# State 11 of a sixteen-state scan is summed in place on VectorE instead of being transposed on TensorE, with all instruction orders laid anew

## The reference

```python
proj = einsum('blh,he->bel', xn, W_in);  hidden, gate = split(proj, 2, axis=1)
hidden = silu(conv(hidden, conv_kernel) + conv_bias)          # 4 taps along the tokens
dt, Bm, Cm = split(einsum('ble,ed->bld', hs_ble, W_x), [128, 144], axis=-1)
dts = softplus(einsum('blr,re->ble', dt, W_dt) + b_dt)
dA  = exp(dts[..., None] * A);   dBu = dts[..., None] * Bm[:, :, None, :] * hs_ble[..., None]
def step(state, inp):                                         # along the 256 tokens
    a, bu, c = inp
    state = a * state + bu
    return state, einsum('ben,bn->be', state, c)              # sum over the 16 states
y = (scan_out + hidden * D) * silu(gate);   ssm = einsum('bel,eh->blh', y, W_out)
# moe: softmax router, top 8 of 32 renormalised; per expert (silu(x @ wg) * (x @ wu)) @ wd * weight
```

## Time and profile before

| | |
|---|---|
| median of three runs | 1346.49 us |
| the profiled execution | 1342.44 us |
| its span, first to last instruction | 1340.6 us |
| PE / PEld busy | 1301.6 / 1219.6 us (97% / 91%) |
| DVE / ACT / POOL busy | 1239.6 / 1213.2 / 1233.9 us (92% / 90% / 92%) |
| mean granted TensorE clock | 0.999 of 2.4 GHz |
| DMA | 130 GB/s mean |

### The profile page before, as it was taken

The page is one execution under the profiler, slowest core; times in us unless marked ns, Lnnn a source line. Parts: engine busy times, 40 slices in busy tenths (PEclk is TensorE's granted clock), DMA queues, the critical chain, the costliest instruction groups (busy, mean ns, idle before and its releaser), DMA issues.

```text
span 1340.6 us, 26644 instructions
## 1 busy us (share of the span) xinstructions
PE 1301.6 (97%) x9222; PEld 1219.6 (91%) x9222; DVE 1239.6 (92%) x1644; ACT 1213.2 (90%) x2111; POOL 1233.9 (92%) x674
## 2 busy tenths in 40 slices
PE   6899999999999999999999999999999999999998
PEld 5889999999999999999999999999999899999987
DVE  3799999999999999999999999999999999999997
ACT  5879999999999999999999999999999899999984
POOL 2999999999999989999999999989999999999996
PEclk9999999999999999999999999999999999999999
DMA  7543443544444344443544444344443534434342
GB/s 193 160 144 118 143 120 115 152 115 132 139 127 135 112 136 127 139 120 118 149 120 126 136 128 138 114 132 131 139 122 116 148 114 134 139 113 142 109 146 80
DMA packets 189399, 174.95 MB, mean 130 GB/s; under 512 B 43185, under 2 KB 172241, under 8 KB 189265
## 3 DMA queue, kind: packets, MB, share of 16 engines
q1 hardware_dynamic: 150864, 121.86, 30.5%
q10 hardware_dynamic: 38400, 51.40, 13.6%
HBM read 167.92 MB, written 5.24 MB: 129 GB/s over the span
## 4 chain that ended last, share of the span: by engine, by line
POOL 27%; issue 21%; ACT 19%; DVE 18%; PE 12%; DMA 2%; ACTq 1%; SPq 0%; DVEq 0%; POOLq 0%
POOL state L571 14%; POOL moe L586 6%; ACT decay L657 5%; PE pair_ps L1003 5%; ACT L657 5%; ACT L665 4%; DVE state L878 4%; PE out_ps L1138 3%; POOL state L580 3%; DVE dt L865 3%; DVE u L891 2%; DVE decay L878 2%; DVE u L919 2%; ACT moe L665 2%; DVE moe L898 2%
## 5 line engine op out<-in xcount | busy, mean ns | idle before, releaser
L571 POOL TENSOR_TENSOR state<-du,b_rep 128x1024 f32<-128x1024 f32 x256 | 611.7, 2395 | 61.1 <-DVE u L891 59.3
L878 DVE TENSOR_TENSOR_SCAN state<-decay,state 128x512 f32<-128x512 f32 x448 | 534.2, 1212 | 21.1 <-ACT decay L657 16.4
L657 ACT ACTIVATE decay<-dt,neg_a 128x255 f32<-128x255 f32 x1024 | 436.7, 465 | 37.7 <-DVE state L878 19.0
L1138 PE MATMUL out_ps<-w_down,moe 128*128 128x256 f32 x1536 | 355.9, 381 | 3.1 <-POOL moe L586 1.9
L1138 PEld LDWEIGHTS out_ps<-w_down,moe 128*128 128x128 f32 x1536 | 282.5, 190 | 38.6 <-issue 4.1
L586 POOL TENSOR_TENSOR moe<-moe,rw_rep 128x512 f32<-128x512 f32 x192 | 249.3, 1309 | 8.7 <-DVE moe L898 7.3
L580 POOL TENSOR_TENSOR state<-state,c_rep 128x1024 f32<-128x1024 f32 x96 | 244.1, 2543 | 1.6 <-DVE state L878 1.6
L1003 PE MATMUL pair_ps<-xnT_hi,w_gate_hi 128*128 128x256 f32 x768 | 228.9, 298 | 3.2 <-DVE moe L898 3.2
L1003 PE MATMUL pair_ps<-xnT_hi,w_up_hi 128*128 128x256 f32 x768 | 225.7, 294 | 2.8 <-ACT moe L665 1.9
L657 ACT ACT_TABLE_LOAD x171 | 219.4, 1283 | 2.5
L1003 PE MATMUL pair_ps<-xnT_lo,w_gate_hi 128*128 128x256 f32 x768 | 216.4, 282 | 0.0
(11 more groups left out here) (149 smaller groups left out, 2252.5 us busy)
## 6 DMA issues: line engine op xcount, KB each, us to landing
w_down<-in_L_ffn_w_down_dram SPq DMA_DIRECT2D x384, 128.0 KB, 2.9
b_rep<-b_dram ACTq DMA_DIRECT2D x128, 256.0 KB, 3.3
rw_rep<-rw_dram SPq DMA_DIRECT2D x256, 96.0 KB, 2.7
c_rep<-b_dram ACTq DMA_DIRECT2D x128, 128.0 KB, 3.3
rw_rep<-rw_dram SPq DMA_DIRECT2D x256, 64.0 KB, 2.6
rw_rep<-rw_dram SPq DMA_DIRECT2D x256, 32.0 KB, 2.6
x_in<-L_attn_input_states_dram SPq DMA_DIRECT2D x16, 256.0 KB, 3.8
res<-L_attn_input_states_dram SPq DMA_DIRECT2D x16, 256.0 KB, 3.1
```

The lines of the kernel that those rows point to most:

```text
L571: pool.tensor_tensor(state[:, n % STATES, :, :], du2[:, q, :, :], b_rep[:, n // BCH % 2, n % BCH, :][:, None, :].broadcast_to([P, ET, T]), ...
L657: last = act.activation(decay[:, h, j, 1:T], dt[:, q, e, 1:T], ACT.Exp, scale=neg_a[:, e, n:n + 1])
L878: dve.tensor_tensor_scan(a if n in ROWS_BY_VECTOR else x, a, x, 0.0, ALU.mult, ALU.add).then_inc(scanned, 1)
L1138: last = pe.matmul(out_ps[:, c, :], moe[:, p % RING, j, c * P:(c + 1) * P], w_down[:, p % RING, j, :], start=(p == 0 and j == 0 and c == 0 ...
```

## The change

State 11 is no longer turned: it joins states 5 and 9 as a row summed by VectorE in the decays' banks. Nine states are then not turned. The code is the same except for the lists; every order table has new numbers. The middle rows (blocks 1 to 14) and the parts for block 0 that are spoken of below:

```diff
-    BY_ROW = [n for n in range(NS) if n in ((2, 4, 5, 6, 8, 9, 10, 12))]
+    BY_ROW = [n for n in range(NS) if n in ((2, 4, 5, 6, 8, 9, 10, 11, 12))]
...
-    UNIT_AT = [[-48, -22, -8, 3, 22, 27, 27, 36, 37, 47, 51, 63, 63, 66, 72, 81, 81, 87, 96, 102, 108, 113, 113, 115],
-               [-3, -2, 4, 23, 26, 30, 30, 35, 36, 42, 45, 49, 49, 52, 55, 81, 85, 95, 101, 104, 108, 108, 114, 115],
...
-    OUT_AT = [[32, 34, 38, 53, 71, 85, 92, 108, 110, 115, 137, 140],
-              [32, 32, 41, 42, 69, 72, 89, 106, 110, 112, 137, 140],
...
-    TURN_AT = [[[1, 8], [23, 27], [28, 31], [68, 68], [95, 104], [105, 111], [114, 114], [117, 119]],
-               [[6, 6], [17, 19], [34, 34], [60, 69], [93, 94], [107, 108], [109, 109], [116, 116]],
...
-    TURN_Y_AT, PROJECT_AT = [[128, 131], [130, 132], [227, 242]], [156, 153, 255]
...
-    SILU_AT = [[-42, -26, 23, 39, 52, 55, 64, 74, 96, 99, 111, 115],
-               [-1, 12, 28, 39, 43, 55, 62, 71, 96, 97, 117, 120],
...
-    SCALAR_FRONT = [{'xnT': -105, 'hid0': -104, 'hid1': -95, 'weightsT': -1, 'low': -65, 'lowT': -49, 'dt0': -41, 'dt1': -35},
-                    {'xnT': -116, 'hid0': -108, 'hid1': -91, 'weightsT': -57, 'low': -50, 'lowT': -41, 'dt0': -40, 'dt1': -23},
...
-    SCALAR_ALONE = [{'conv_silu': -74, 'router_exp': -94, 'softplus': -29, 'first_state': 4, 'skip': -9, 'normed': -123, 'share': -45},
-                    {'conv_silu': -73, 'router_exp': -84, 'softplus': -20, 'first_state': 7, 'skip': 23, 'normed': -122, 'share': -62},
...
-    MUL_AT = [[-10, 13, 41, 55, 60, 67, 79, 85, 108, 112, 118, 124],
-              [14, 23, 41, 46, 59, 63, 79, 92, 107, 108, 127, 129],
...
-    ADD_AT = [[[23, 26], [58, 71], [81, 97], [104, 113], [113, 117], [121, 124], [126, 129]],
-              [[20, 22], [64, 65], [84, 98], [104, 105], [114, 116], [120, 126], [130, 131]],
...
-    ROW_ADD_AT = [[42, 54, [45, 47], 70, 80, [76, 79], 106, 116], [37, 49, [44, 47], 61, 78, [76, 76], 102, 119], [30, 51, [43, 44], 64, 78, [75, 76], 102, 153]]
-    VECTOR_ALONE = [{'stats': -127, 'lo': -99, 'logits': -57, 'route': -37, 'taps0': -80, 'taps1': -53, 'total': 162},
-                    {'stats': -125, 'lo': -107, 'logits': -79, 'route': -71, 'taps0': -98, 'taps1': -83, 'total': 165},
...
-    SUM_AT = [[136, 136], [135, 136], [201, 214]]
...
-    WEIGH_AT = [[25, 26, 36, 43, 56, 65, 73, 94, 102, 110, 135, 136],
-                [17, 29, 37, 44, 65, 66, 80, 91, 99, 103, 131, 133],
...
-    ROW_MUL_AT = [[17, 30, [44, 44], 42, 63, [75, 78], 86, 91], [21, 32, [43, 45], 55, 67, [72, 76], 90, 92], [12, 30, [42, 44], 49, 67, [73, 76], 89, 116]]
-    POOL_ALONE = [{'rstd': -120, 'step_input': -35, 'gated': 142, 'select': -95},
-                  {'rstd': -127, 'step_input': -17, 'gated': 140, 'select': -66},
...
-    C_LOAD_AT = [[-11, 7, 26, 43, 44, 62, 69, 86], [-10, -10, 26, 40, 41, 61, 70, 80], [-22, -22, 31, 43, 57, 63, 82, 92]]
-    ROWS_BY_VECTOR = [n for n in BY_ROW if n in ((5, 9))]
+    UNIT_AT = [[-63, -27, -15, -7, 8, 18, 27, 42, 42, 44, 51, 51, 57, 57, 65, 74, 76, 76, 89, 90, 92, 99, 110, 114],
+               [-5, -4, -2, 16, 21, 24, 37, 37, 39, 51, 51, 52, 58, 61, 74, 75, 93, 94, 101, 102, 102, 111, 114, 122],
...
+    OUT_AT = [[29, 32, 49, 56, 61, 67, 85, 97, 99, 112, 139, 140],
+              [32, 40, 41, 65, 67, 77, 83, 97, 109, 112, 141, 142],
...
+    TURN_AT = [[[6, 10], [14, 15], [17, 31], [63, 74], [104, 107], [111, 112], [120, 123]],
+               [[5, 6], [15, 16], [30, 32], [73, 74], [104, 108], [111, 112], [118, 122]],
...
+    TURN_Y_AT, PROJECT_AT = [[125, 126], [126, 126], [227, 231]], [148, 145, 245]
...
+    SILU_AT = [[-38, -18, 27, 36, 44, 44, 63, 70, 86, 87, 108, 116],
+               [-1, 14, 37, 38, 47, 52, 70, 70, 96, 97, 118, 120],
...
+    SCALAR_FRONT = [{'xnT': -114, 'hid0': -104, 'hid1': -97, 'weightsT': -11, 'low': -66, 'lowT': -58, 'dt0': -38, 'dt1': -28},
+                    {'xnT': -114, 'hid0': -105, 'hid1': -90, 'weightsT': -55, 'low': -46, 'lowT': -42, 'dt0': -39, 'dt1': -28},
...
+    SCALAR_ALONE = [{'conv_silu': -77, 'router_exp': -81, 'softplus': -26, 'first_state': 16, 'skip': 16, 'normed': -124, 'share': -13},
+                    {'conv_silu': -84, 'router_exp': -78, 'softplus': -18, 'first_state': 6, 'skip': 26, 'normed': -124, 'share': -62},
...
+    MUL_AT = [[-26, -7, 35, 45, 57, 59, 75, 80, 97, 109, 119, 125],
+              [12, 23, 46, 50, 60, 63, 80, 88, 104, 109, 124, 129],
...
+    ADD_AT = [[[25, 28], [61, 64], [103, 116], [119, 119], [120, 125], [127, 127]],
+              [[21, 23], [62, 76], [99, 102], [116, 116], [116, 119], [128, 132]],
...
+    ROW_ADD_AT = [[41, 53, [43, 45], 61, 87, [73, 79], 95, [92, 94], 118], [38, 51, [44, 47], 61, 78, [76, 77], 100, [91, 94], 118], [39, 50, [42, 45], 61, 79, [72, 78], 95, [93, 93], 158]]
+    VECTOR_ALONE = [{'stats': -118, 'lo': -75, 'logits': -70, 'route': -53, 'taps0': -75, 'taps1': -58, 'total': 167},
+                    {'stats': -126, 'lo': -107, 'logits': -73, 'route': -68, 'taps0': -100, 'taps1': -81, 'total': 161},
...
+    SUM_AT = [[133, 133], [133, 135], [233, 246]]
...
+    WEIGH_AT = [[18, 25, 29, 39, 54, 59, 73, 76, 96, 104, 133, 135],
+                [13, 29, 37, 44, 55, 67, 74, 87, 100, 106, 136, 136],
...
+    ROW_MUL_AT = [[9, 28, [41, 44], 46, 70, [72, 78], 76, [88, 94], 103], [26, 29, [44, 44], 45, 65, [73, 77], 75, [89, 93], 95], [20, 28, [42, 44], 44, 57, [72, 76], 84, [90, 93], 183]]
+    POOL_ALONE = [{'rstd': -93, 'step_input': -21, 'gated': 138, 'select': -18},
+                  {'rstd': -128, 'step_input': -21, 'gated': 139, 'select': -74},
...
+    C_LOAD_AT = [[-32, -9, 28, 42, 48, 54, 73, 78, 89], [17, 25, 31, 41, 54, 59, 72, 78, 89], [7, 15, 34, 38, 57, 62, 70, 79, 103]]
+    ROWS_BY_VECTOR = [n for n in BY_ROW if n in ((5, 9, 11))]
...
-    SPLIT_SCALAR_AT = [-115, -104, -102, -86, -73, -68, -51, -44, -41, -30, -28, -13, -7, -3, 0, 0, 10, 18]
...
+    SPLIT_SCALAR_AT = [-127, -97, -90, -90, -75, -61, -61, -52, -33, -28, -25, -15, -10, -5, -4, 5, 13, 13]
```

More of the change, by code:

```diff
@@ new lines, in build @@
+    PE_FRONT = [{'xnT': -118, 'hid0': -108, 'hid1': -93, 'logits': -92, 'weightsT': 3, 'low': -70, 'lowT': -69, 'dt0': -61, 'dt1': -51},
+                {'xnT': -120, 'hid0': -112, 'hid1': -100, 'logits': -79, 'weightsT': -61, 'low': -53, 'lowT': -50, 'dt0': -40, 'dt1': -34},
+                {'xnT': -119, 'hid0': -112, 'hid1': -102, 'logits': -82, 'weightsT': -59, 'low': -53, 'lowT': -50, 'dt0': -35, 'dt1': -33}]
+    GATE_AT = [[55, 64], [51, 59], [95, 161]]
+    SILU_AT = [[-38, -18, 27, 36, 44, 44, 63, 70, 86, 87, 108, 116],
+               [-1, 14, 37, 38, 47, 52, 70, 70, 96, 97, 118, 120],
+               [-2, 29, 34, 36, 47, 54, 68, 77, 87, 87, 209, 237]]
@@ new lines, in build @@
+    SCALAR_FRONT = [{'xnT': -114, 'hid0': -104, 'hid1': -97, 'weightsT': -11, 'low': -66, 'lowT': -58, 'dt0': -38, 'dt1': -28},
+                    {'xnT': -114, 'hid0': -105, 'hid1': -90, 'weightsT': -55, 'low': -46, 'lowT': -42, 'dt0': -39, 'dt1': -28},
+                    {'xnT': -114, 'hid0': -108, 'hid1': -91, 'weightsT': -53, 'low': -48, 'lowT': -40, 'dt0': -34, 'dt1': -21}]
+    SCALAR_ALONE = [{'conv_silu': -77, 'router_exp': -81, 'softplus': -26, 'first_state': 16, 'skip': 16, 'normed': -124, 'share': -13},
+                    {'conv_silu': -84, 'router_exp': -78, 'softplus': -18, 'first_state': 6, 'skip': 26, 'normed': -124, 'share': -62},
+                    {'conv_silu': -59, 'router_exp': -78, 'softplus': -18, 'first_state': 18, 'skip': 6, 'normed': -124, 'share': -65}]
```

31 lines of the change are left out of this document (12 added, 19 removed).

## The result

Four runs of the changed kernel take 1369.55 us in the median (1368.92 to 1370.67), four runs of the kernel before beside them 1345.96. The ratio is 1.018, with a 95% interval of 1.016 to 1.020: the change costs 24 us where 4.4 us of gain were forecast. The profiled execution took 1369.5 us, its span is 1367.7.

What follows compares the result with a forecast made beforehand. GpSimd with its row sums was taken as the bound. 15 x -0.35 = -5.25, +1.25 at the start and -0.4 at the end gave -4.4 us: 1342.1 us from 1346.49, range 1334 to 1356.

Steps and rivals of the forecast that it cites:

- The bound: Middle blocks: GpSimd's own 75.69 us plus 3.7 for three row sums it idles for, 79.4 of 80.40 us.
- The counts: Per block: TensorE loses eight transposes (0.87 us), VectorE gains 1.27 us, ScalarE's table loads fall from 22 to 18.
- The walk: Middle blocks' new lists, walked with the trace's durations: row sum 8 ends at 51.8 us, the period becomes 80.05.
- Rival (a): VectorE bounds the part behind row sum 8, state 11's additional 1.1 us on the path: +17 in full, 1364 us; chance 0.18.
- The gain of 0.35 a period: Middle blocks: GpSimd's slack falls from 1.0 to 0.65 us, so the period becomes 80.05; 15 x -0.35 = -5.25 us.
- The first part: First scan to end of row sum 8: has to fall from 54.3 to 52.5 us, forecast to end at 51.8.
- The second part: End of row sum 8 to the next block's first scan: VectorE's work without a gap, from 26.2 to 27.9 us.
- rival (b): Nothing gained: GpSimd's slack stays about 1.0 us, only the ends differ; 1347 us, chance 0.18.
- Waits that are late anyway.: Per block: ScalarE's one more row load stands behind waits that are late anyway, so it was costed at nothing.
- The start: Before the first block's softplus: a second weight split and the wait for stored B rows make it 1.25 us later.
- Block 0 and the end: Block 0 without a term; at the end half of TensorE's 0.87 us saved, -0.4 us.

Runs made afterwards that it cites:

- race_won: The changed kernel with state 3's second accumulating addition on VectorE moved from slot 76 to 70 in blocks 1 to 14; 1354.9 us.
- small_product11: The changed kernel with VectorE's two multiplications of state 11 by row C cut from 256 to 8 columns of each group; 1371.0 us.
- feed_and_race: load11_early with the router weights' eviction and store before state 10's decays, and eviction `low` behind those of state 11's second half; 1350.1 us.
- fed_small11: feed_and_race with VectorE's two multiplications of state 11 by row C cut to 8 columns of each group; 1346.9 us.
- load11_early: race_won with the load of state 11's row C issued at slot 72 and not 78 in blocks 1 to 14; 1358.6 us.
- low_later: load11_early with the low-rank projection's two evictions on ScalarE moved behind the decays of states 11 and 12; 1373.5 us.

## Why the prediction was wrong, step by step

- **The bound.** "75.69 us of its own and six row sums, 79.4 of 80.40" describes the kernel before well. But it treats the lock as time that is only added up. In the changed kernel GpSimd waits 4.4 us a period on VectorE's multiplications and scans, and the sum stays 2.6 us under the period.
- **The counts.** Eight transposes, 1.27 us for VectorE and the table loads stood as worked out: 144 loads before decays and 101 before SiLUs of pairs, for 171 and 144 before (groups of the changed kernel, columns as there).

```profile
L657 ACT ACT_TABLE_LOAD x144 | 184.8, 1283 | 2.1
...
L665 ACT ACT_TABLE_LOAD x101 | 129.6, 1283 | 5.0 <-issue 2.0 <-PE out_ps L1138 1.4
```

- **The walk: the step that failed.** "Row sum 8 ends at 51.8, 0.7 better than needed." From the first scan (376.25) it is issued at 50.56 and ends at 54.0. The walk's times are good: product 2 ends at 21.3 as it says, scan 4 at 22.1 (21.7) and row sum 2 at 23.2 (22.9), and 51.8 less the row sum's own 1.23 is 50.57. What it had wrong is who holds the lock at that time: it gave row sum 8 its plain 1.2 us, and VectorE came 0.01 us after GpSimd had begun the input of state 11. The loss is 2.2 us. race_won shows it from the other side: issued at 50.1, while GpSimd still weighs pair 5, the row sum gets in and ends at 51.7, just as the walk said. The walk printed its margins as if being late by d cost d. Ahead of an exclusive lock it costs the length of the instruction that gets in first.
- **Rival (a)** had the right point of decision ("later than 52.5 after the first scan"), a chance of 0.18 and the nearest size (+17 in full; 24 measured). Its two parts even add up: 54.0 and the 27.9 that the forecast counted behind row sum 8 are the 81.96 of the period. That is luck in part, for its mechanism was another one: it priced VectorE's 1.1 us of added work. small_product11 takes this work away and the loss stays. With the lock won the work is worth 0.23 us a period.
- **The gain of 0.35 a period.** Not there even with the lock won and the row and store mended: 80.42 against 80.49 before. The first part came out: row sum 8 ends at 51.7 from the first scan, with 51.8 forecast. In it product 4 waits 0.89 us and lasts 0.88 longer, with row sum 2's own 1.2 us inside, so 0.57 us are lost beyond it, where the walk allowed 0.45. The second part, from there to the next first scan, takes 28.7 us; the forecast's period of 80.05 left it 28.25. There the weighing of pair 6 waits 0.4 to 0.5 us in thirteen of the fourteen periods, nearly always for its multiplication; a wait like the 0.29 at product 10 stands in the period shown alone.

```profile
392.83 3.25 POOL L580 TENSOR_TENSOR state<-state,c_rep 128x1024 f32<-128x1024 f32 x1 [0.89 <-DVE state L878]
...
425.02 1.26 POOL L586 TENSOR_TENSOR moe<-moe,rw_rep 128x512 f32<-128x512 f32 x1 [0.42 <-DVE moe L898]
426.57 2.37 POOL L580 TENSOR_TENSOR state<-state,c_rep 128x1024 f32<-128x1024 f32 x1 [0.29 <-DMA c_rep<-b_dram]
```

(GpSimd's timeline in feed_and_race.) What makes the second part 0.45 us longer than forecast is not shown; fed_small11, with 1.1 us less for VectorE there, takes only 0.2 off it. GpSimd's slack didn't close, it moved: rival (b), 1347, describes what feed_and_race's periods reach, not its start and end.
- **"Waits that are late anyway."** The load of row C 11 was costed at nothing because the wait ahead of it hides it. That cover was the lost lock: when it went, in race_won, the product waited 1.76 us for the row.
- **The start.** +1.02 us against 1.25, by a step that the forecast named: ScalarE's `dt1` waits for the stored B rows, since the first load of B stands before it now (ScalarE's timeline after):

```profile
34.28 0.84 ACT L695 ACTIVATE dt<-turn_ps,b_dt 128x256 f32<-128x256 f32 x2 [1.23 <-DMA b_dram<-bcT]
```

- **Block 0 and the end** were taken as unchanged and as -0.4; they are +2.7 and +2.8 us. At the end the new order has TensorE wait for a scan before the transposes of states 13 and 14, with the last pairs queued behind, where the old one had no wait over 0.3 us (TensorE's timeline after):

```profile
1346.01 1.09 PE L1100 MATMUL turn_ps<-ident,state 128*128 128x128 f32 x8 [1.68 <-DVE state L878]
```

Ahead of it stands one more lost lock, of the last block's row sum 10 (VectorE's, then GpSimd's row after); GpSimd's next input then waits 1.23 us for it. Before, no row sum of the last block takes over 2.22 us. In block 0, row sum 2 lasts 3.17 us (1.39 before). How much of the two losses these make is not shown.

```profile
1337.35 3.53 DVE L891 TENSOR_TENSOR u<-u,state 128x1024 f32<-128x1024 f32 x1
```

```profile
1337.37 2.43 POOL L571 TENSOR_TENSOR state<-du,b_rep 128x1024 f32<-128x1024 f32 x1
```

The last block's lists were not walked, only its last wait was read. The median lies 24 us above that of before and not 27 as the spans do: the runs spread by a few us, and the profiled execution of before is among its fastest.

## What to carry to other kernels

Where two engines exclude each other, an order is not robust against 0.1 us: look in the forecast for each place where both become ready within a few tenths of each other, and price the losing branch in full, with what is queued behind the loser. Make sure of such a place by moving a small independent instruction into an idle gap ahead of it; here one number out of several hundred was worth 24 us. After such a move look at the other places again: load11_early and low_later won the lock at row sum 8 and lost it at row sum 12. An instruction costed at nothing "because something else is later" has to be walked again once that something is gone.
